# A chain of eight transformer layers on one core: ternary weights made by GpSimd alone, expert rows in another order

## What is computed

```python
def ternary_quant(w_fp32, g=GROUP_SIZE):           # GROUP_SIZE = 64
    w = w_fp32.astype(jnp.bfloat16)
    w_g = w.reshape(-1, g)
    scale = jnp.clip(jnp.mean(jnp.abs(w_g), axis=-1, keepdims=True), 1e-08, None)
    q = jnp.clip(jnp.round(w_g / scale), -1, 1)
    w_hat = (q * scale).reshape(w.shape)
    return w + jax.lax.stop_gradient(w_hat - w)
...
probs = jax.nn.softmax((x @ gate_w.T).astype(jnp.float32), axis=-1)
top_w, top_i = jax.lax.top_k(probs, TOP_K)         # TOP_K = 2, 8 experts
...
for e in range(E):
    h = jax.nn.silu(x @ w1[e].T) * (x @ w3[e].T)
    out = out + w_dense[:, e:e + 1] * (h @ w2[e].T)
```

## Time and profile before

| | |
|---|---|
| median of three runs | 838.62 us (838.59 to 839.54) |
| the profiled execution | 836.64 us, its span 834.8 us |
| busy of the span | TensorE 77%, VectorE 61%, ScalarE 34%, GpSimd 30% |
| mean granted clock of TensorE | 0.88 of full speed |
| chain that ended last | TensorE 50%, VectorE 20%, "issue" 7%, DMA 3%, GpSimd 3% |
| channel stage | 296 to 414 us |
| expert stage | 547 to 835 us, its loop 581 to 818 us |

### The profile page before, as it was taken

One profiled execution on the slowest core, in us unless ns is written; L12 is line 12 of the kernel. 1 busy time (PEld: TensorE's weight loads), 2 busy tenths in 40 slices (PEclk: granted clock), 3 DMA queues, 4 the chain that ended last, 5 costly groups with the idle time before them and its releaser, 6 DMA issues.

```text
span 834.8 us, 10906 instructions
## 1 busy us (share of the span) xinstructions
PE 640.8 (77%) x3645; PEld 406.1 (49%) x3660; DVE 505.4 (61%) x1092; ACT 284.7 (34%) x519; POOL 247.5 (30%) x247
## 2 busy tenths in 40 slices
PE   1632888875785268889968999852999999999991
PEld 1322345543464114555545667541566666666661
DVE  7998988755978999999767455944122222222223
ACT  4811533213446304667853223610112112211110
POOL 3211243147930188455032014001022111111100
PEclk9885999867977557999999999955999999999997
DMA  7002202000112641654120002995000100000005
GB/s 253 0 0 75 89 1 53 12 1 0 40 25 46 121 105 29 160 156 112 53 78 0 1 1 83 429 427 194 7 32 25 31 26 25 25 25 25 19 13 165
DMA packets 34141, 61.83 MB, mean 74 GB/s; under 512 B 6233, under 2 KB 29785, under 8 KB 31769
## 3 DMA queue, kind: packets, MB, share of 16 engines
q1 hardware_dynamic: 24992, 48.93, 18.7%
q0 software_dynamic: 2208, 6.03, 2.3%
q10 hardware_dynamic: 6896, 6.29, 2.2%
HBM read 47.35 MB, written 13.50 MB: 73 GB/s over the span
## 4 chain that ended last, share of the span: by engine, by line
PE 50%; DVE 20%; issue 7%; DMA 3%; POOL 3%; ACT 1%; POOLq 0%; SPq 0%; DVEq 0%; ACTq 0%
PE bank L1810 17%; PE bank L1831 8%; DVE region L1181 4%; PE bank L1419 4%; PE bank L1440 3%; PE bank L1104 2%; PE bank L556 2%; PE bank L1821 2%; DMA norm_rows<-XN 2%; PE bank L1064 2%; PE bank L528 2%; PE bank L1088 2%; DVE XN L357 1%; DVE wide L1168 1%; PE bank L1945 1%
## 5 line engine op out<-in xcount | busy, mean ns | idle before, releaser
L1810 PE MATMUL bank<-region,wide 128*128 x368 | 145.2, 548 | 0.3 <-issue 0.3
L1710 DVE TENSOR_TENSOR wide<-wide,bank 128x448 f32<-128x448 f32 x46 | 28.6, 621 | 128.5 <-ACT wide L1754 128.5
L1810 PEld LDWEIGHTS bank<-region,wide 128*128 128x128 f32 x368 | 69.3, 194 | 62.3 <-issue 62.3
L1181 DVE TENSOR_REDUCE region<-bank 128x2 f32<-128x512 f32 x128 | 80.4, 679 | 4.6 <-PE bank L1064 4.3
L1127 ACT ACTIVATE region<-bank 128x1024 f32<-128x1024 f32 x64 | 63.1, 1025 | 48.6 <-PE bank L1088 48.5
L1616 POOL DMA_INDIRECT choice_results<-wide,to_row x23 | 22.8, 990 | 181.5 <-DVE wide L1723 181.5
L1831 PE MATMUL bank<-region,XN 128*128 x322 | 73.4, 379 | 1.2 <-DVE wide L1723 1.2
L1064 PE MATMUL bank<-region 128*128 128x256 bf16 x256 | 53.4, 309 | 19.2 <-DVE region L1181 14.4
L1831 PEld LDWEIGHTS bank<-region,XN 128*128 128x128 f32 x322 | 59.5, 190 | 9.3 <-issue 2.1
L1754 ACT ACTIVATE wide<-bank 128x448 f32<-128x448 f32 x46 | 25.0, 544 | 113.4 <-PE bank L1810 113.4
L371 POOL TENSOR_TENSOR rstd<-vareps,half_neg 128x4 f32<-128x4 f32 x16 | 17.4, 1085 | 128.0 <-DVE vareps L367 128.0
(11 more groups left out here) (302 smaller groups left out, 1225.6 us busy)
## 6 DMA issues: line engine op xcount, KB each, us to landing
region<-in_L_ffn_experts_dram SPq DMA_DIRECT2D x8, 2688.0 KB, 23.4
region<-ctx_parts SPq DMA_DIRECT2D x24, 192.0 KB
region<-norm_parts SPq DMA_DIRECT2D x24, 192.0 KB
channel_values<-wide ACTq DMA_DIRECT2D x8, 512.0 KB, 5.1
ctx_parts<-region SPq DMA_DIRECT2D x40, 64.0 KB, 2.1
region<-in_L_ffn_w_gate_up_dram SPq DMA_DIRECT2D x4, 512.0 KB, 6.6
wide<-channel_values SPq DMA_DIRECT2D x16, 128.0 KB, 2.6
norm_parts<-region SPq DMA_DIRECT2D x24, 64.0 KB, 4.2
```

What stands on the lines that cost most here:

```text
L1181: e.tensor_reduce(nmax[i % 2][:, at_:at_ + KC], score_bank("scores", n).rearrange("p (c n) -> p c n", c=KC), AX.X, ALU.max, negate=True).t ...
L1710: e.tensor_tensor(HB8[par][:, cols], silu8[:, cols], bank[hf][:, 512:512 + I8 // 2], ALU.mult)\
L1810: last = e.matmul(bank[hf][:, 512 * gu:512 * gu + hw], xbT[par][:, P * c:P * c + P], region[:, bass.ds(off + (2 * gu + c) * I8 + hw * hf, ...
```

## The change

**Ternary weights.** VectorE's two comparisons per chunk are gone, and with them the thresholds. Near 96 us VectorE takes the reciprocal of the scales (`tinv`) instead, times a factor that puts the rounding boundary where the comparison had it. In the channel stage GpSimd alone makes the chunk: product with `tinv` in f32, a tensor_scalar with minimum and addition of a large number (which rounds), a tensor_scalar with maximum and subtraction, and then the product with the scale, the subtraction and the addition as before. It waits once, for the scales.

```diff
@@ vec_ternary_sums
-                e.tensor_scalar(thigh, tscb, 0.5 + 2.0 ** -9, None, ALU.mult)
-                ch.link(e.tensor_scalar(tlow, tscb, -(0.5 + 2.0 ** -9), None, ALU.mult))
+                ch.link(e.reciprocal(tinv, tscb))
+                e.tensor_scalar(tinv, tinv, 0.5 / (0.5 + 2.0 ** -9), None, ALU.mult).then_inc(s_tern["weights_summed"], 1)
@@ vec_ternary_signs is gone, and pair_steps of VectorE no longer calls it
-                e.tensor_tensor(by_group(tpos[c % 2]), by_group(w), spread(thigh[:, g]), ALU.is_gt)
-                e.tensor_tensor(by_group(tneg[c % 2]), by_group(w), spread(tlow[:, g]), ALU.is_lt).then_inc(s_tern["weights_signs"], 1)
@@ pool_ternary_weights
-            e.wait_ge(s_tern["weights_signs"], c + 1)
-            ch.link(e.tensor_tensor(pos, pos, neg, ALU.subtract))
-            ch.link(e.tensor_tensor(by_group(pos), by_group(pos), spread(tscb[:, g]), ALU.mult))
-            ch.link(e.tensor_tensor(pos, pos, w, ALU.subtract))
-            e.tensor_tensor(w, w, pos, ALU.add).then_inc(s_tern["weights_ternary"], 1)
+            ch.link(e.tensor_tensor(by_group(tquot), by_group(w), spread(tinv[:, g]), ALU.mult))
+            ch.link(e.tensor_scalar(tquot, tquot, 1.0, MAGIC, ALU.min, ALU.add))
+            ch.link(e.tensor_scalar(tsign, tquot, MAGIC - 1.0, MAGIC, ALU.max, ALU.subtract))
+            ch.link(e.tensor_tensor(by_group(tsign), by_group(tsign), spread(tscb[:, g]), ALU.mult))
+            ch.link(e.tensor_tensor(tsign, tsign, w, ALU.subtract))
+            e.tensor_tensor(w, w, tsign, ALU.add).then_inc(s_tern["weights_ternary"], 1)
```

```diff
@@ results_in
-                            ys_dram[N * k + 2 * P * j:N * k + 2 * P * (j + 1), :].rearrange("(t p) d -> p t d", p=P))\
+                            ys_dram[N * k:N * k + N, :].rearrange("(p t) d -> p t d", t=NT)[:, 2 * j:2 * j + 2, :])\
@@ pool_experts
-            ch.link(e.iota(tile_base, [[P, 2 * NT]], base=0, channel_multiplier=0, allow_small_or_imprecise_dtypes=True))
-            ch.link(e.iota(lane_1, [[0, 1]], base=1, channel_multiplier=1, allow_small_or_imprecise_dtypes=True))
+            ch.link(e.iota(tile_1, [[0, 2], [1, NT]], base=1, channel_multiplier=0, allow_small_or_imprecise_dtypes=True))
+            ch.link(e.iota(lane_rows, [[N, 2]], base=0, channel_multiplier=NT, allow_small_or_imprecise_dtypes=True))
...
-            e.wait_ge(s_moe["norm_stored"], 16)
+            e.wait_ge(s_moe["norm_stored"], 32)
@@ vec_experts
-            ch.link(e.tensor_scalar(hi_hot[:, :, 0, :], hi_hot[:, :, 0, :], lane_1, None, ALU.mult))
+            for k in range(2):
+                last = e.tensor_scalar(hi_hot[:, NT * k:NT * k + NT, 0, :], hi_hot[:, NT * k:NT * k + NT, 0, :],
+                                       lane_rows[:, k:k + 1], None, ALU.mult)
+            ch.link(last)
@@ act_experts
-            leave_half(XT8, 0, 6, s_turn, s_turned, base=TURN["moe"])
-            leave_half(XT8, 1, 0, s_turn, s_turned, base=TURN["moe"])
+            for hf in range(2):
+                e.wait_ge(s_xn, 7 * NT + 4 * (hf + 1))
+                e.dma_start(xn_dram.rearrange("(p t) d -> p t d", t=NT)[:, 4 * hf:4 * hf + 4, :],
+                            XN[:, 4 * D * hf:4 * D * hf + 4 * D].rearrange("p (t d) -> p t d", d=D))\
+                    .then_inc(s_moe["norm_stored"], 16)
+                leave_half(XT8, hf, (6, 0)[hf], s_turn, s_turned, base=TURN["moe"])
             e.wait_ge(s_moe["logits_shifted"], 1)
             e.activation(route["ex"], route["lg"], ACT.Exp).then_inc(s_moe["logits_exp"], 1)
-            e.wait_ge(s_xn, 8 * NT)
-            e.dma_start(xn_dram.rearrange("(t p) d -> p t d", p=P), XN[:, :].rearrange("p (t d) -> p t d", d=D))\
-                .then_inc(s_moe["norm_stored"], 16)
```

28 lines of the change are left out of this document (8 added, 20 removed).

## The result

The changed kernel takes **835.12 us** (median of 6 runs, 833.32 to 835.39) where the kernel before took 838.61 beside it (6 runs, 835.89 to 841.38): a ratio of 0.9949, 95% interval 0.9926 to 0.9971. It is faster, by 3.5 us in place of the 16.95 that were forecast, and lies outside the range of 817.5 to 827.5. The profiled execution has a span of 833.4 us and took 835.33. Among the runs of before beside the later experiments, two took 946 and 948 us at a mean granted clock of 0.71, a slower state, and the ratios leave them out.

A forecast was written before the change was run, and what follows sets the result against it. VectorE, with TensorE nearly level, was taken to bound the channel stage, and the norm-row store the experts' start. Terms -7.0 - 7.65 + 0.5 - 2.3 - 0.5 = -16.95 us gave 821.7 from 838.62, range 817.5 to 827.5.

The forecast's parts named there:

- part 2: Channel stage, GpSimd's six operations a chunk: 10.6 us each, 64 for six, ending at 375, hidden before TensorE turns the weights.
- rival (b): Channel stage: GpSimd becomes the bound, TensorE's turning of weights waits; 843 us at p = 4.5 per tensor_scalar; chance 0.08.
- Part 1, opening: Opening of the channel stage: without VectorE's comparisons the second value group comes 7.0 us earlier, bounds 3.5 and 7.5.
- Steady part: Channel stage, 40 pairs: eight pairs take 12.17 us in place of 13.70, so 7.65 us go, bounds 6.5 and 8.5.
- Is VectorE slowed by GpSimd?: Channel stage: no; eight reductions took 5.08 us both beside GpSimd and without it.
- Part 2, reciprocal: VectorE near 96 us, before the first attention's gate selection: a reciprocal replaces a tensor_scalar, +0.5 us, bounds 0 and 0.7.
- Part 3: Start of the experts: norm rows stored early by halves no longer hold the first gather, -2.3 us, bounds 0 and -2.6.
- Part 4: Final reads, rows numbered lane by lane: 2 KB pieces make the first pair land sooner, -0.5 us, bounds 0 and -1.2.
- rival d: TensorE's clock at the first expert slot and two or three other places: may move by 1.7 us either way.
- (a): TensorE takes VectorE's place sooner, gather waits for weights, tail gives nothing: 9.5 us gained, 829.1; chance 0.12.
- (c): The quotients change nothing on the path, TensorE being bound everywhere; only parts 3 and 4 act: 836.3 us; chance 0.02.

The follow-up runs named there:

- quick forms: Changed kernel with GpSimd's two slow tensor_scalars per chunk written as three (min with max, then mult with add twice), same result to the bit: 819.41 us, ratio 0.9809.
- fast_whole: Kernel with the quick forms, rows still numbered lane by lane, but norm rows stored in one piece behind the router's exponentials: 822.33 us, ratio 0.9805.
- the rows alone: Kernel before with only norm rows leaving by halves, expert rows numbered lane by lane and final reads in 2 KB pieces: 837.00 us beside 837.67, ratio 0.9982.
- the second profile: The changed kernel run once more, nothing altered: 834.80 us, ratio 0.9950.

## Why the prediction was wrong

**The step that failed** is in part 2, "No GpSimd tensor_scalar is in the trace. Nearest is a one-input cast ... I take 1.04". The price was 3.64 us. The prediction had the mechanism as rival (b), with its condition: late above p = 2.7 us, gain gone above 4.1. By its own formula 311 + 51 + 12 x 3.64 = 405.7, 11.0 us late, 832.7 us; the stage entered 4 us late by the clock, and TensorE's clock fell while it waited, and it was 835.1. The range should have taken this in: the rows named a far end (the power) and the sum of the bounds stopped at 2.12, because every row below it was a tensor_tensor or a cast. The price was of another kind of instruction, so rows of neighbours did not bound it; 0.08 was too little for it. With the quick forms, three operations at the very 1.04 that was assumed for two, the time is 819.4 where 821.7 was forecast; the terms below missed by about a microsecond each, both ways.

**Part 1, opening: the first step right, the clock's share not.** The second value group comes at 324.60 us in place of 328.66, with the stage entered 4.0 us late: 8.0 gained in place of 7.0, 0.5 over the upper bound. The turned scores start 2.5 us sooner, as was said. But the prediction let the clock rise at the same instant, 317.3. It did so (317.5), but only because the stage was late: counted from VectorE's last variance ahead of the stage, the rise comes after 24.4 to 24.9 us in the four profiles with the comparisons and after 20.9 to 21.2 in the eleven without them. And before, the clock was low once more from 320.8 to 327.6 us, which the prediction did not see; none of the eleven has such a stretch. The windows of before and of the changed kernel:

```profile
321.00:328.00 7.00, 6.38 (x38) 3.32 (x39) 5.68 (x13) 1.81 (x3) 6.84 (x4) 0.53 0.02 4
```

```profile
321.00:328.00 7.00, 6.63 (x77) 4.17 (x81) 6.79 (x15) 5.09 (x7) 6.84 (x3) 1.00 0.03 6
```

**Steady part: right.** From that group to the twentieth behind it, 324.60 to 385.43, it is 60.83 us where it was 68.49: -7.66, and -7.65 was forecast. Over the eleven profiles without the comparisons it lies between -5.4 (fast_whole) and -7.66 (four of them), so the size is right and the match to a hundredth is not to be expected again. TensorE is 97% busy there (67.1 of 69 us), not 91%.

**Is VectorE slowed by GpSimd?** The reductions are not: the eighteen of the opening ran back to back in 10.8 us beside a busy GpSimd. The comparisons, with two inputs from SBUF, were, and this the prediction did not look at. Those of the earlier trace rows that ran beside GpSimd's two-input operations took 2.08 and 1.86 us, the last, beside nothing, 1.13. GpSimd was slowed too: in the timeline of before, one line of the code beside a comparison and alone:

```profile
316.82 2.98 POOL L1263 TENSOR_TENSOR region<-region 128x1024 bf16<-128x1024 bf16 x1
...
326.99 2.12 POOL L1263 TENSOR_TENSOR region<-region 128x1024 bf16<-128x1024 bf16 x1
```

So of the 6.4 us that the prediction read off the chain, some 1.7 are there because the two engines held each other up.

**Part 2, reciprocal: right in size.** It takes 0.75 us, and VectorE's work behind it is 0.4 later by 101 us.

**Part 3: the sum near, the reason wrong.** -2.3 was forecast, 0.15 for the added operation taken in. From the row numbers to TensorE's first work on the gathered rows it is 3.0 us less with the rows alone and 2.0 less in the changed kernel, 0.5 of it because the gather follows the row numbers by 0.3 us and not by GpSimd's 0.83. The step "the store, 7 and 14 us earlier, is past before 572.45" credits the early issue; in small pieces the early halves land after the row numbers. What failed is that credit: in larger pieces the same 512 KB are down in 12 us. "The bytes are the same, so this end stays" held with the rows alone (the engines empty from 573 on); in the changed kernel the weights end later, and beside them its first gather reaches TensorE 4.2 us after its start (4.3 in the second profile), with the rows alone 3.2. **Part 4: wrong in sign.** The final reads in 2 KB pieces cost 0.7 to 0.9 us in place of giving 0.5; full engines say nothing of when the first of eight reads lands.

**The clock (rival d)** moved more than allowed: 1 to 6 us between 98 and 165 us, in profiles of any of these kernels. Rivals (a) and (c) did not come: the comparisons on VectorE were worth all that was said.

## What to carry to other kernels

Before work moves to an engine, measure the exact instruction there, with its pair of operations and types; a neighbour's price does not bound it, and a range must reach to the point where the engine becomes the bound. On GpSimd write tensor_scalars as min with max or mult with add where you can, even if that takes one more instruction or a multiplication by 1. A store that competes with large loads gets through by large pieces, not by an early issue.

## What the runs showed of the hardware

- GpSimd, 1024 elements a lane: tensor_scalar with min and max or mult and add 1.04 us, as a copy; a single add, subtract or mult 2.77 to 2.85; min with add, max with subtract 3.64. Types and the place of the constant hardly matter. The Trainium skill, page GPSIMD Engine Reference, section "Engine selection", calls one-input work roughly line rate; the first kind agrees, and the others are 2.7 and 3.5 times that.
- The same 512 KB stored beside the expert weights: 12 to 13 us in 4 KB pieces, 26 to 31 in 1 KB pieces; 1 MB in 8 KB pieces 13.7, in 1 KB pieces 17.4 and 20.2. In 1 KB pieces a store was down only when the weights had run out, whenever it was issued.
- A comparison on VectorE and a two-input operation on GpSimd slowed each other: the one took 1.86 to 2.08 us in place of 1.13, the other 2.98 in place of 2.12. VectorE's reductions out of PSUM were not slowed.
- TensorE's granted clock fell to half (1.2 GHz) while it waited 11.3 us (low from 402.9 to 413.1), and was low again from 426.8 to 437.0, where before it was low from 426.6 to 430.0.
- One kernel's runs lie up to 8.7 us apart (834.75 to 843.42 over the runs of before), and where the clock is low between 98 and 165 us is one source of it.
